# A timetable of the Mamba stage: dt and output products, C's turn, gates and z's SiLUs at other slots

## The chip, the core and the metric

The kernel runs on one NeuronCore of a Trainium2 chip. The metric is the device time of one launch in microseconds (us). Five engines work side by side, each through its own instruction stream in order, and meet only through semaphores: TensorE (PE in the views; matmuls and transposes into the eight banks of PSUM), VectorE (DVE), ScalarE (ACT), GpSimd (POOL) and SyncE (SP, which here only issues DMAs, its queue being SPq). The Mamba stage's data is fp32.

## The reference, cut to what matters

The input is x, 2 sequences of 4096 tokens by 256. It is normalised and modulated and goes through a Mamba layer forward and one backward in time; both results pass a sigmoid, are averaged, normalised and added to the residual; then an FFN with ternary weights follows. The Mamba layer is what the change touches:

```
xi, z = split(x @ in_proj.T)                 # 512 channels each
xi    = silu(causal_conv(xi) + conv_b)
dt, B, C = split(xi @ x_proj.T)              # 64, 16, 16 columns
dt    = softplus(dt @ dt_w.T + dt_b)
dA, dBx = exp(dt * A), dt * xi * B           # for each of 16 states
h     = dA * h + dBx                         # along time
y     = (sum over states of h * C) + xi * D
out   = (y * silu(z)) @ out_proj.T
```

## The kernel before, in words

The Mamba stage runs 32 bodies: two passes (backward, then forward in time) of 16 chunks, a chunk being 512 tokens of one sequence; chunks of the two sequences take turns. After it comes the FFN stage (from line 1497 on), which the change leaves alone.

A body has 32 **units** k. Units 0 to 15 are the 16 states of the first half of the channels, 16 to 31 those of the second half; a unit has two tiles m of 128 channels by 512 tokens. A body thus has 64 **slots** g = 2k + m. Each engine walks the slots in order, and beside the scan work of chunk n it does the front work of chunk n+1 and the tail work of chunk n-1, each piece at the slot that a table gives. The tables are written out by hand at the top of the file, `AT` (lines 43 to 50) for TensorE's slots, with fixed lags for the readers: ScalarE reads a front product `ACT_LAG` = 3 slots after its last step, VectorE gates `DVE_LAG` = 2 slots after the turn.

The scan work of a unit:

- ScalarE makes the decay exp(dt * A) of each tile (`decay`, L1145), into one of three PSUM banks; a decay of tile i waits until scan i-3 is over. Units 19, 22, 25, 28 and 31 (`A_UNITS`) are the other way about: the decay goes to SBUF, and the share dBx comes from TensorE as a product with a diagonal matrix (`fill_a`, L815), at slots 2k-2 and 2k-1.
- GpSimd makes dBx of the other units (`weigh_b`, L1283).
- VectorE scans (`scan`, L1400), a tile at a time.
- Four units later h is weighed with C: 12 units on GpSimd (L1294), 20 on VectorE (L1408); for these TensorE first spreads C over the partitions (`spread_c`, L850) into a single bank, which needs the weighing before it to be over.
- Five units later TensorE turns h and sums it over the states in PSUM (`turn_h`, L868). At the end of each half it adds xi * D (`turn_skip`, L880) and ScalarE copies the sum to `acc` (`evacuate`, L1099; slot 44 for the first half). The turn of the next unit waits for both copies.

The pieces that the tables place, with their jobs in two PSUM banks (`FB`, numbers in `BANK`), each job waiting until its bank's last job has been read:

- `J_X`, `J_CONV`, `J_B`: x part of in_proj, convolution, x_proj. ScalarE copies them; `xi_silu` (L1060) makes two SiLUs of 128x1024 at slots 24 and 31 (`AT_XI`).
- `J_C`: turn of B and C (L783), read by ScalarE (L1041) 3 slots later.
- `J_DT`: four dt products (L731), read by ScalarE twice each (L1048, L1049); then exp and ln at slots 48, 49, 53, 54.
- `J_Z`: z part of in_proj, copied by ScalarE (L1026) for the next chunk; `z_silu` (L1087) makes its SiLU for the chunk being scanned, at `AT_ZS`.
- `J_Y`: turn of `acc` to channels (L724), gated by VectorE with silu(z) (`gate`, L1377): two tiles for the first half of the channels, two (at slots 13 and 17 of the next body) for the second.
- `J_OUT`: two output products of four quarters each (`tail`, L835), one quarter a slot; ScalarE reads each with a tanh (L1111) 6 slots after it began; SP stores the chunk when both are read.

The exp and Silu functions lie in different table sets, so an ACT_TABLE_LOAD stands wherever ScalarE changes between them. Within a slot ScalarE does the decay first, then tail, then front, then xi's SiLU, then z's. Within a slot TensorE does spread and turn of h, then tail, the turns of y and u, `fill_a`, then front. The first chunk's front is made in a prologue of 64 slots of its own, where z's products stand at `FIRST_Z`.

Of the kernel before, what the change touches and what calls it, by code (L numbers as in the profile page):

```python
# [39 lines left out]
J_LN, J_X, J_CONV, J_B, J_DT, J_Z = (0, 1), (2, 3, 4, 5), (6, 7, 8, 9), 10, (11, 12, 13, 14), (15, 16, 17, 18)  # L40
J_Y, J_OUT, J_C = (19, 20, 21, 22), (23, 24), 25
J_UT = (26, 27)
AT = {J_LN: (0, 1), J_X: (3, 5, 7, 9), J_CONV: (11, 16, 20, 24), J_DT: (35, 40, 43, 49), J_Z: (50, 52, 56, 57),
      J_Y: (46, 47, 13, 17), J_OUT: (32, 38), J_UT: (26, 29)}
AT_LN, AT_X, AT_CONV, AT_DT, AT_Z, AT_Y, AT_OUT, AT_UT = (AT[j] for j in (J_LN, J_X, J_CONV, J_DT, J_Z, J_Y, J_OUT, J_UT))
AT_B, AT_C = 29, 37
NFB = 2
BANK = (0, 1, 0, 1, 0, 1, 0, 1, 0, 1, 1, 1, 1, 1, 1, 0, 1, 0, 1, 1, 0, 1, 0, 0, 0, 1, 0, 0)
START = {J_B: AT_B, J_C: AT_C, **{j: g for jobs, gs in AT.items() for j, g in zip(jobs, gs)}}
FIRST_Z = (33, 46, 38, 52)  # L50
FIRST_START = {**START, **dict(zip(J_Z, FIRST_Z))}
AT_ROWS = (16, 21, 26, 30, 32, 37, 41)
R_MOD, R_BANK = 3, 1
# [14 lines left out]
ND, NP = len(D_UNITS), len(P_UNITS)  # L68
ACT_LAG, DVE_LAG = 3, 2
EVAC = (44, 12)  # L70
AT_XI, AT_ZS = (24, 31), (5, 62)
AT_XN = 19
AT_EXP = (48, 53)
AT_LNP = (49, 54)
# [281 lines left out]
def mamba(nc, a, bank, ident, cols, mod, gain, norm_c, fcol, any_odd, passes, w1, w2, J, x_v, yb_v, yf_v, xn_v, b_dram,  # L356
# [11 lines left out]
    with ExitStack() as c:  # L368
# [46 lines left out]
        def job(ch, i):  # L415

            b = BANK[i]

            def count(jobs):
                return sum(BANK[k] == b for k in jobs)

            def before(jobs, start=START):
                return sum(BANK[k] == b and start[k] < start[i] for k in jobs)

            nf, nm, nt = count(FRONT), count(MID), count(TAIL)
            back = 1 if i in FRONT else 0 if i in MID else -1
            n = ch.number()
            body = None if n is None else n - back  # L430
            if body == -1:
                return b, before(FRONT, FIRST_START)
            more = len(AT_ROWS) if b == R_BANK and (body == NALL or body == NALL - 1 and i in MID) else 0
            off = nf - nt + before(MID) + before(TAIL) + before(FRONT)
            if body == 0:
                off += nt - before(TAIL)
            if body == NALL - 1:
                off -= before(FRONT)
            if body == NALL:
                off = -nt + before(TAIL)  # L440
            return b, ch.at(nf + nm + nt, off - back * (nf + nm + nt) + more)

        def row_job(e):

            last = Chunk(NPASS - 1, NC - 1, 1)
            return job(last, next(i for i in MID if BANK[i] == R_BANK))[1] - len(AT_ROWS) + e

        def wait_filled(eng, ch, i):
            b, k = job(ch, i)
            eng.wait_ge(fill[b], k + 1)  # L450
# [268 lines left out]
        def _(pe):  # L719
            def turn(i, src, ch):  # L720

                wait_free(pe, ch, i)
                for s in range(TS):
                    mm = pe.transpose(FB[BANK[i]][:, s * P:(s + 1) * P], src(s), ident[:, :])  # L724
                mm.then_inc(fill[BANK[i]], 1)

            def part(ch, i, k, kn, lhsT, rhs, rows=P):

                if k == 0:
                    wait_free(pe, ch, i)  # L730
                mm = pe.matmul(FB[BANK[i]][0:rows, :], lhsT, rhs, start=(k == 0), stop=(k == kn - 1))  # L731
                if k == kn - 1:
                    mm.then_inc(fill[BANK[i]], 1)

            def front(ch, g):
# [10 lines left out]
                for m in range(KI):  # L746
# [20 lines left out]
                    if g == AT_DT[m]:  # L767
                        if m == 0:
                            wait_drained(pe, ch, J_B)
                        part(ch, J_DT[m], 0, 1, w_dt[:, m * P:(m + 1) * P], dbB[0:DTR, :])  # L770
                    k = g - (FIRST_Z if ch.first() else AT_Z)[m]
                    if 0 <= k < KM:
# [201 lines left out]
        def _(act):  # L974
            def front(ch, g):
# [25 lines left out]
                for m in range(KI):  # L1001
# [15 lines left out]
                    if g == AT_CONV[m] + DCONV - 1:  # L1017
# [4 lines left out]
                                       bias=cv[:, COL_CB + m:COL_CB + m + 1]).then_inc(drain[b], 1)  # L1022
                    if g == (FIRST_Z if ch.first() else AT_Z)[m] + KM - 1:
                        wait_filled(act, ch, J_Z[m])
# [798 lines left out]
```

## Time and profile before

| | us |
|---|---|
| median of 3 runs (lowest, highest) | 4886.2 (4885.44, 4889.81) |
| profiled execution | 4887.08 |
| its span, first to last instruction | 4885.3 |
| mean granted TensorE clock | 0.984 |

| engine | busy us | share of the span |
|---|---|---|
| TensorE matmul | 4500.2 | 92% |
| VectorE | 3896.9 | 80% |
| GpSimd | 3321.8 | 68% |
| ScalarE | 3277.3 | 67% |

The Mamba stage fills about the first 3545 us. A row of a timeline shows: start, duration, engine, line, operation, tiles, and how many instructions in a row it merges; in brackets the idle time before it and who ended that. The next instruction may start up to 0.2 us before the end of the one before it, so the distance of two starts (the stride) is a little less than the duration.

### The profile page before, as it was taken

The numbers are of one execution on the slowest core, as the hardware profiler recorded it, in microseconds if no ns is written. First come the engines' busy times: TensorE is split into PE (matmuls) and PEld (weight loads), VectorE is DVE, ScalarE is ACT, GpSimd is POOL, SyncE is SP. The second block draws the span as 40 slices with busy tenths as digits, with TensorE's granted clock in tenths as the row PEclk, the third lists the DMA queues.
The fourth block names the chain that finished last, engine by engine and source line by source line (L and its number), as shares of the span: only waits on it lengthen the run. The fifth ranks groups of instructions, "written<-read, shape, count | busy, mean of one in ns | idle before, by whom it ended". The sixth has DMA issues, their size and how long they took to land. (4 is left out here: it accounts for less than half of the span.)

```text
span 4885.3 us, 67229 instructions
## 1 busy us (share of the span) xinstructions
PE 4500.2 (92%) x24932; PEld 3377.8 (69%) x24932; DVE 3896.9 (80%) x4126; ACT 3277.3 (67%) x5281; POOL 3321.8 (68%) x1559
## 2 busy tenths in 40 slices
PE   7899889999889889999999999999789999999999
PEld 3666666666666666666666666666678888888888
DVE  6999999999999989999999999999855444545452
ACT  7877777777777777777777777777534444444443
POOL 5999999999999999998999999989920000000000
PEclk9999999999999999999999999999999999999999
DMA  8544444444444444444444444444430101011000
GB/s 287 171 135 130 149 129 130 123 138 136 129 141 137 139 126 131 134 131 126 134 141 129 127 129 126 133 137 131 141 124 31 35 31 35 31 33 33 29 28 9
DMA packets 297737, 545.77 MB, mean 112 GB/s; under 512 B 101888, under 2 KB 186624, under 8 KB 262784
## 3 DMA queue, kind: packets, MB, share of 16 engines
q1 hardware_dynamic: 296512, 529.91, 35.7%
q10 hardware_dynamic: 896, 11.54, 0.7%
q8 instruction: 199, 3.26, 0.3%
q14 instruction: 130, 1.06, 0.1%
HBM read 502.77 MB, written 50.14 MB: 113 GB/s over the span
## 5 line engine op out<-in xcount | busy, mean ns | idle before, releaser
L1400 DVE TENSOR_TENSOR_SCAN m_h<-bank,m_state,m_dBx 128x512 f32<-128x512 f32 x1512 | 1847.7, 1263 | 34.0 <-ACT bank L1145 27.8
L868 PEld LDWEIGHTS bank<-ident,m_h 128*128 128x128 f32 x8192 | 982.6, 144 | 627.4 <-issue 373.8
L868 PE MATMUL bank<-ident,m_h 128*128 128x128 f32 x8192 | 1246.8, 279 | 117.2 <-DVE m_h L1408 84.7
L1294 POOL TENSOR_TENSOR m_h<-m_h,m_Cs 128x1024 f32<-128x1024 f32 x384 | 909.5, 2373 | 214.9 <-ACT m_state L1077 214.8
L1283 POOL TENSOR_TENSOR m_dBx<-u,m_Bs 128x1024 f32<-128x1024 f32 x432 | 1013.8, 2376 | 2.4 <-issue 0.6
L1283 POOL TENSOR_TENSOR m_dBx<-m_u,m_Bs 128x1024 f32<-128x1024 f32 x432 | 1013.1, 2372 | 3.4 <-DMA m_Bs<-b_dram 1.3
L1408 DVE TENSOR_TENSOR m_h<-m_h,bank 128x1024 f32<-128x1024 f32 x640 | 765.1, 1195 | 14.6 <-PE bank L850 14.4
L1145 ACT ACTIVATE bank<-m_dt,cols 128x512 f32<-128x512 f32 x864 | 588.8, 688 | 218.8 <-DVE m_h L1400 215.5
L1145 ACT ACTIVATE bank<-dt,cols 128x512 f32<-128x512 f32 x864 | 588.8, 688 | 200.0 <-DVE m_h L1400 196.7
L302 POOL TENSOR_TENSOR mvj<-mvj,norm_c 128x4 f32<-128x4 f32 x16 | 16.2, 1015 | 983.4 <-DVE mvj L263 983.4
L850 PEld LDWEIGHTS bank<-ident,m_Ct 128*128 128x128 f32 x2560 | 300.1, 140 | 529.9 <-DVE m_h L1408 350.5
L850 PE MATMUL bank<-ident,m_Ct 128*128 128x128 f32 x2560 | 411.3, 285 | 221.2 <-DVE m_h L1408 219.1
L731 PE MATMUL bank<-hT,w_in 128*128 128x512 f32 x1024 | 522.4, 599 | 7.8 <-ACT hT L998 4.1
L731 PE MATMUL bank<-xpre,diag 128*128 128x512 f32 x1024 | 524.4, 596 | 0.0
L1588 PE MATMUL bank<-gb,h 128*128 128x512 f32 x2048 | 468.3, 390 | 0.0
L1588 PE MATMUL bank<-ga,h 128*128 128x512 f32 x2048 | 467.9, 389 | 0.0
L1400 DVE TENSOR_TENSOR_SCAN m_h<-m_h,m_state,bank 128x512 f32<-128x512 f32 x280 | 350.9, 1269 | 144.9 <-ACT bank L1145 84.5
L1588 PEld LDWEIGHTS bank<-ga,h 128*128 128x128 f32 x2048 | 384.3, 188 | 80.8 <-DVE ga L1726 0.3
L1588 PEld LDWEIGHTS bank<-gb,h 128*128 128x128 f32 x2048 | 383.3, 188 | 78.9
L1726 DVE TENSOR_TENSOR ga<-raw,ga 128x512 fp32r<-128x512 f32 x256 | 178.2, 696 | 302.2 <-ACT raw L1663 300.8
L815 PE MATMUL bank<-m_dg,m_uT 128*128 128x128 f32 x2560 | 340.3, 276 | 0.0
L815 PEld LDWEIGHTS bank<-m_dg,m_uT 128*128 128x128 f32 x2560 | 313.3, 193 | 0.0
(176 smaller groups left out, 6003.3 us busy)
## 6 DMA issues: line engine op xcount, KB each, us to landing
m_Bs<-b_dram SPq DMA_DIRECT2D x256, 1024.0 KB, 5.2
m_Cs<-c_dram SPq DMA_DIRECT2D x384, 256.0 KB, 3.5
m_dg<-d_dram SPq DMA_DIRECT2D x160, 256.0 KB, 3.6
xx<-in_x SPq DMA_DIRECT2D x16, 512.0 KB, 4.9
xn_dram<-xx SPq DMA_DIRECT2D x16, 512.0 KB, 4.6
yb_dram<-m_ysb SPq DMA_DIRECT2D x16, 512.0 KB, 4.4
xx<-xn_dram SPq DMA_DIRECT2D x16, 512.0 KB, 3.8
x_dram<-m_ysb SPq DMA_DIRECT2D x16, 512.0 KB, 4.4
```

What stands on the lines that cost most here:

```text
L302: pool.tensor_tensor(mvj[:, :, 3], mvj[:, :, 2], norm_c[:, 1, :], ALU.pow).then_inc(S["join"], 1)
L731: mm = pe.matmul(FB[BANK[i]][0:rows, :], lhsT, rhs, start=(k == 0), stop=(k == kn - 1))
L815: mm = pe.matmul(DA[tile % NDA][:, s * P:(s + 1) * P], uT[:, s, m * P:(m + 1) * P], dg[:, n % NDG, s, :], start=True, stop=True)
L850: mm = pe.matmul(CB[:, t * P:(t + 1) * P], Ct[:, ch.batch, t, s:s + 1].broadcast_to((P, P)), ident[:, :], start=True, stop=True, is_transp ...
L868: mm = pe.matmul(YB[b][:, o:o + P], h[:, k % NH, m, tok:tok + P], ident[:, :], start=(s == 0 and o == 0), stop=False, is_transpose=True, s ...
L1145: act.activation(out, dt[ch.batch][:, m, :], ACT.Exp, scale=cols[:, ch.ps, col:col + 1]).then_inc(S["da"], 1)
L1283: pool.tensor_tensor(dBx[:, dbx_ring(ch, k) % NDBX, :, :], u[ch.batch][:, m, :], Bs[:, k // BP % 2, k % BP, :].unsqueeze(1).broadcast_to(( ...
L1294: pool.tensor_tensor(o, o, Cs[:, i % 2, :].unsqueeze(1).broadcast_to((P, 2, T)), ALU.mult).then_inc(S["weigh_p"], 1)
L1400: dve.tensor_tensor_scan(o, decays, share, initial, ALU.mult, ALU.add).then_inc(S["scan"], 1)
L1408: dve.tensor_tensor(o, o, CB[:, :].unsqueeze(1).broadcast_to((P, 2, T)), ALU.mult).then_inc(S["weigh_d"], 1)
L1588: return pe.matmul(out, lhsT, rhs, start=start, stop=stop)
L1726: dve.tensor_tensor(dst[:, 1], raw[:, j % XR, :], dst[:, 0].bitcast(F32), ALU.subtract).then_inc(S["lo"], 1)
```

## The change

It alters tables only. In a body: the first output product moves from slot 32 to 33 and the second from 38 to 44; the third dt product from 43 to 42 and the fourth from 49 to 46; C's turn from 37 to 38; the turns of the first half's y from 46 and 47 to 60 and 61, and with them VectorE's first two gates from 48 and 49 to 62 and 63; the second dt product uses bank 0 instead of 1; z's SiLUs move from slots 5 and 62 to 24 and 31, where xi's are. In the prologue the first chunk's second and third z products move from 46 and 38 to 48 and 37.

```diff
-AT = {J_LN: (0, 1), J_X: (3, 5, 7, 9), J_CONV: (11, 16, 20, 24), J_DT: (35, 40, 43, 49), J_Z: (50, 52, 56, 57),
-      J_Y: (46, 47, 13, 17), J_OUT: (32, 38), J_UT: (26, 29)}
+AT = {J_LN: (0, 1), J_X: (3, 5, 7, 9), J_CONV: (11, 16, 20, 24), J_DT: (35, 40, 42, 46), J_Z: (50, 52, 56, 57),
+      J_Y: (60, 61, 13, 17), J_OUT: (33, 44), J_UT: (26, 29)}
...
-AT_B, AT_C = 29, 37
+AT_B, AT_C = 29, 38
 NFB = 2
-BANK = (0, 1, 0, 1, 0, 1, 0, 1, 0, 1, 1, 1, 1, 1, 1, 0, 1, 0, 1, 1, 0, 1, 0, 0, 0, 1, 0, 0)
+BANK = (0, 1, 0, 1, 0, 1, 0, 1, 0, 1, 1, 1, 0, 1, 1, 0, 1, 0, 1, 1, 0, 1, 0, 0, 0, 1, 0, 0)
 START = {J_B: AT_B, J_C: AT_C, **{j: g for jobs, gs in AT.items() for j, g in zip(jobs, gs)}}
-FIRST_Z = (33, 46, 38, 52)
+FIRST_Z = (33, 48, 37, 52)
...
-AT_XI, AT_ZS = (24, 31), (5, 62)
+AT_XI, AT_ZS = (24, 31), (24, 31)
```

## Rows read from the trace of the kernel before

**Rows 1.** The page's slices: VectorE's busy tenths in 40 slices.

```profile
DVE  6999999999999989999999999999855444545452
```

**Rows 2.** Timeline of VectorE over one body; columns as told above.

```profile
2027.21 2.45 DVE L1400 TENSOR_TENSOR_SCAN m_h<-bank,m_state,m_dBx 128x512 f32<-128x512 f32 x2
...
2068.68 1.28 DVE L1400 TENSOR_TENSOR_SCAN m_h<-bank,m_state,m_dBx 128x512 f32<-128x512 f32 x1 [0.48 <-ACT bank L1145]
...
2080.31 2.45 DVE L1400 TENSOR_TENSOR_SCAN m_h<-bank,m_state,m_dBx 128x512 f32<-128x512 f32 x2
...
2088.90 1.22 DVE L1408 TENSOR_TENSOR m_h<-m_h,bank 128x1024 f32<-128x1024 f32 x1 [0.31 <-PE bank L850]
2090.26 2.58 DVE L1400 TENSOR_TENSOR_SCAN m_h<-m_h,m_state,bank 128x512 f32<-128x512 f32 x2
...
2101.80 2.58 DVE L1400 TENSOR_TENSOR_SCAN m_h<-m_h,m_state,bank 128x512 f32<-128x512 f32 x2 [3.13 <-ACT bank L1145]
...
2106.06 1.28 DVE L1400 TENSOR_TENSOR_SCAN m_h<-bank,m_state,m_dBx 128x512 f32<-128x512 f32 x1 [0.50 <-ACT bank L1145]
...
2109.56 0.67 DVE L1377 TENSOR_TENSOR m_z<-bank,m_z 128x512 f32<-128x512 f32 x1
...
2111.92 2.44 DVE L1400 TENSOR_TENSOR_SCAN m_h<-m_h,m_state,bank 128x512 f32<-128x512 f32 x2
...
2129.42 1.25 DVE L1400 TENSOR_TENSOR_SCAN m_h<-m_h,m_state,bank 128x512 f32<-128x512 f32 x1
2132.53 1.28 DVE L1400 TENSOR_TENSOR_SCAN m_h<-m_h,m_state,bank 128x512 f32<-128x512 f32 x1 [1.87 <-ACT m_h L1145]
...
2134.84 2.45 DVE L1400 TENSOR_TENSOR_SCAN m_h<-bank,m_state,m_dBx 128x512 f32<-128x512 f32 x2
```

**Rows 3.** Timeline of TensorE over the same body.

```profile
2084.83 1.03 PE L835 MATMUL bank<-m_w_out,m_z 128*128 128x256 f32 x4
...
2086.13 1.03 PE L835 MATMUL bank<-m_w_out,m_z 128*128 128x256 f32 x4
2087.09 1.12 PE L731 MATMUL bank<-m_dbB,m_w_dt 64*128 64x512 f32 x2
2088.14 0.65 PE L850 MATMUL bank<-ident,m_Ct 128*128 128x128 f32 x4
...
2089.07 1.06 PE L815 MATMUL bank<-m_dg,m_uT 128*128 128x128 f32 x8
...
2100.11 0.66 PE L868 MATMUL bank<-ident,m_h 128*128 128x128 f32 x4 [0.60 <-ACT m_acc L1099]
2100.60 1.06 PE L815 MATMUL bank<-m_dg,m_uT 128*128 128x128 f32 x8
...
2134.98 1.11 PE L850 MATMUL bank<-ident,m_Ct 128*128 128x128 f32 x4 [3.61 <-DVE m_h L1408]
```

**Rows 4.** Timeline of ScalarE over the body of rows 2.

```profile
2065.58 1.06 ACT L1060 ACTIVATE m_xi<-m_u 128x1024 f32<-128x1024 f32 x1
2066.66 1.28 ACT L1145 ACT_TABLE_LOAD   x1
2067.96 1.30 ACT L1145 ACTIVATE bank<-dt,cols 128x512 f32<-128x512 f32 x2
...
2079.47 0.69 ACT L1145 ACTIVATE bank<-dt,cols 128x512 f32<-128x512 f32 x1
...
2097.22 0.69 ACT L1048 ACTIVATE m_u<-bank,cols 128x512 f32<-128x512 f32 x1 [2.48 <-PE bank L731]
...
2098.99 1.07 ACT L1099 COPY m_acc<-bank 128x512 f32<-128x512 f32 x2
```

**Rows 5.** Timeline of SP's DMA queue over the same body.

```profile
2117.39 7.54 SPq L577 DMA_DIRECT2D m_Bs<-b_dram  x2
```

**Rows 6.** Timeline of GpSimd over the same body.

```profile
2129.35 6.97 POOL L1283 TENSOR_TENSOR m_dBx<-m_u,m_Bs 128x1024 f32<-128x1024 f32 x3
```

**Rows 7.** Timeline of TensorE, a body of the first pass.

```profile
1077.29 0.65 PE L850 MATMUL bank<-ident,m_Ct 128*128 128x128 f32 x4 [1.70 <-DVE m_h L1408]
```

## The prediction

> **What bounds the kernel now.** I read the page's shares first, then the timelines of VectorE, TensorE and ScalarE over one steady body (one chunk, 32 units of two scans, 64 slots g; slot 2k is the first half of unit k), then SP's and GpSimd's. The shares over the span hide two stages: VectorE's slices are at nine tenths nearly all through the Mamba stage and at four or five in the FFN stage behind it [rows 1], which isn't touched. So the body's length is what counts: VectorE's first scan of two successive bodies stands at 2027.21 and 2134.84, 107.6 us apart [rows 2]. VectorE's own work in it is 64 scans at a stride of 1.18, 20 weighings at 1.12 and 4 gates at 0.58, 100.2 us. The rest is five waits and small gaps behind them [rows 2]: 0.48 at 2068.68 (slot 25), 0.31 at 2088.90 with some 0.2 before 2090.26 (slots 37, 38), 3.13 at 2101.80 (slot 44), 0.50 at 2106.06 (slot 47), 1.87 at 2132.53 (slot 63). The view puts the 3.13 down to ScalarE's decay, but that is unit 22, whose share comes from a TensorE fill; this fill runs 2100.60 to 2101.66 [rows 3], and the scan starts 0.14 behind it. So slot 44 is TensorE's: the fill is late because of the products ahead of it in its order, the last wait before it being 0.60 for ScalarE's copies of acc. Slots 25 and 63 are ScalarE's: two table loads of 1.28 around a Silu of 1.06 hold the next decay back [rows 4]. A change is worth what it takes off these five, less the waits that it makes.
>
> **Part 1, z's SiLUs.** Slot 5's block (load, Silu, load) goes. VectorE doesn't wait there, so it brings 0. Slot 62's goes: VectorE's two scans of unit 31 stand 3.11 apart (2129.42, 2132.53) and need 1.18, so 1.93 comes back. At slots 24 and 31 z's Silu now follows xi's directly: I take no table load between them, so the block grows by one Silu, 1.06 less the 0.10 by which such instructions overlap, 0.96. At slot 24 VectorE waits already, so all of it is path: +0.96. At slot 31 the decay starts at 2079.47, lasts 0.69 and the scan starts at 2080.31 [rows 2, 4]: cover 0.1 at most, +0.91. Unit 16 starts 1.87 later than now. Bounds of the two together: 0.9 (the second hidden) to 7.0 (with 1.28 of loads kept on both sides of each Silu), taken 1.87, from the chain just read. ScalarE saves four loads, 5.1 us a body, beside other work. Here the load at 2066.66 lasts 1.28 and the next decay runs at 2067.96, 1.30 behind it [rows 4]. The Trainium skill's page "ScalarE: Activation LUTs", section "What ACT_TABLE_LOAD costs", adds a drain of 1.38 us to each load; by it ScalarE would save 10.7 us a body instead of 5.1 and the block at slot 24 would be about 6 us instead of 3.6 long. The trace does not agree, and decides.
>
> **Part 2, output and dt products before unit 19 (slots 32 to 38).** The first output product moves from slots 32-35 to 33-36. Its last quarter now stands between unit 14's spread and unit 19's fill. TensorE must first turn unit 12, whose weighing ends two scans and itself after unit 16's start: 2080.31 + 1.87 + 2.38 + 1.19 = 2085.75. From 2085.81 TensorE does: turn 0.49, quarter 0.86, turn 0.44, quarter 0.96, dt 1.05, spread 0.49, turn 0.44, quarter 0.86, in all 5.59 [rows 3] (strides: 2084.83 to 2086.13 for a quarter and a turn, 2086.13 to 2087.09, 2087.09 to 2088.14, 2088.14 to 2089.07). The fill starts at 2091.40, ends 2092.46, unit 19 is scanned from 2092.59 instead of 2090.26: +2.33. The 0.31 at slot 37 vanishes in this. Bounds: +1.6 (VectorE alone) to +2.4.
>
> **Part 3, slots 38 to 44.** C's turn goes from 37 to 38 (0.33 us, TensorE idle follows: 0). The second output product leaves slots 38-41, four quarters of 0.87, so TensorE is at the end of slot 41 about 2098.2 in spite of the lateness; it no longer bounds. What is late next is ScalarE: unit 20's first scan runs 2095.09 to 2096.3, decay 43 takes 0.62 to 2097.00, the dt product's two reads and decay 44 take 1.77 (2097.22 to 2098.99) [rows 4], the two acc copies 1.07, to 2099.84. TensorE resumes at 2099.89, not 2100.11. Unit 22 is scanned from 2101.58 instead of 2101.80: **-0.22**. So of the 3.5 us taken off TensorE nearly all pays for the 2.33.
>
> **Part 4, slots 42 to 50.** The third dt product comes to slot 42, between unit 22's two fills: the second fill starts 0.99 + 1.05 + 0.49 = 2.53 behind the first (2102.91, end 2103.97), the second scan at 2104.09, where now it is at 2103.10 (+0.99). ScalarE's reads at slot 45 are done by 2103.7, so the 0.50 at slot 47 goes. VectorE could start unit 25 at 2104.09 + 1.20 + 2.36 + 1.12 + 2.36 = 2111.13, the gates having left. But TensorE has, from 2102.91: fill 0.89, two turns and two quarters 2.60, spread 0.44, turn 0.43, quarter 0.96, dt 1.05, turn 0.49, quarter 0.86, turn 0.44, 8.16: fill of unit 25 2111.07 to 2112.13, scan 2112.26, the second 2113.58, unit 26 at 2114.78 against 2114.28 (2111.92 + 2.36): **+0.50**. ScalarE's decay 50 ends at 2111.8 behind the fourth dt reads, just hidden. Bounds: 0 to +1.2 (decay 50 late by 0.7).
>
> **Part 5, slots 50 to 63.** The gates stay two of 0.58, at slots 62 and 63 now; 1.17 is paid there, and 1.17 saved at 48 and 49 is in part 4. Their turns are ready, at slots 60 and 61. These add 0.87 to TensorE ahead of unit 31's second fill; I get the fills' ends at 2129.6 and 2131.4 and the scans at 2129.92 and 2131.70, hidden by 0.2. Next body: 2129.92 + 1.20 + 0.58 + 1.18 + 0.59 + 1.11 = 2134.58, now 2134.84: **-0.26 a body**. Bounds: that to +0.9, if TensorE is 0.8 later. The second output tile is read at slot 50 rather than 44, so SP, which issues in order, sends the store of y at some 2112.1, and behind it queue a C load, a diagonal load, the four diagonal stores and the next B load, which goes from 2117.39 to about 2118.9; GpSimd needs it at 2129.35 [rows 5, 6]. Hidden: 10 us less a landing of 5.2 by the page. The second dt product's other bank makes it wait for the first output tile's read, which is over 3 us before: 0. The first chunk's z products move by a slot or two in the prologue, where I give 0, with bounds of -2 and +2 us once.
>
> **Sum.** 31 bodies at -0.3 (the -0.26, and a trifle at slot 5) are -9.3; the last body, where TensorE's tail work is what VectorE waits for, -2. From the profiled execution, 4887.1 (span 4885.3 and 1.8 around it), that is 4875.8; from the median, 0.9 lower, **4875**. About 0.2%, 9.8 us, is what can be told from no change, so the likeliest case lies on this edge. The parts are differences of large terms: 1 us a body is 31 us.
>
> **Rivals.** *A: TensorE's relief counts in full.* If the SiLUs' lateness is absorbed ahead of unit 22 and the fills of 22 and 25 come in time: -2.5 at slot 44, -0.5 at 47, -1.9 at 63, +1.9, -3.0 a body, 4793. For it: the largest wait is TensorE's. Against it: the ScalarE chain and the third dt product above. Half of it gives 4835.
> *B: ScalarE's chain through decay 43, the dt reads and the acc copies decides.* From the acc copies' end TensorE runs with no break to unit 25, so each tenth of lateness there goes straight to the body's end. It is 0.22 ahead now; from 0.04 behind on the kernel is slower. If it comes 1 us later than worked out (another instruction of ScalarE in the chain, or turns at 60 and 61 that hold unit 31's fills): +0.7 a body, 4908. For it: all margins here are below 0.5. Against it: each link is a row.
> *C: TensorE's clock falls at new places.* After an idle of 3.61 four transposes took 1.11 (1.2 GHz), after one of 1.70 0.65 (2.4 GHz) [rows 3, 7]. The new idle stretches at slots 34 and 42 are 1.3 and 1.6. If they too let it fall, 3 us of path a body: 4975.
> *D: the two moves only exchange waits*, within 0.1 us a body: 4883 to 4889.
>
> **Chances.** Forecast (4860 to 4880) 0.34, A and half of it 0.16, D and the forecast's weak side 0.26, B 0.21, C 0.03. Range 4838 to 4912. Faster 0.48, same 0.29, slower 0.23.
>
> **What would show it.** In a steady body: no table load at slots 5 and 62; VectorE's wait at slot 25 near 1.4 and a new one near 0.9 at slot 32; about 1 us at slot 38, 0.65 at slot 44, 1.3 at 45, 1.1 at 50; no wait at 47 or 63; TensorE's clock low less often at the body's start, where its idle shrinks from 3.6 to about 1.5. The prediction is wrong if the wait at slot 32 is absent, if slot 44's stays over 1 us, or if a body is more than 1 us away from 107.3.

## The result, and the profile after

The changed kernel takes 4989.36 us (median of 4 runs, 4984.14 to 4993.17) against 4887.32 before (4 runs): a ratio of 1.0208, 95% interval 1.019 to 1.0225. It is 102 us slower, where 12 us faster was forecast, and outside the range of 4838 to 4912. The profiled execution has a span of 4989.7 us. From the page after:

```profile
PE 4511.3 (90%) x24932; PEld 3354.8 (67%) x24932; DVE 3903.8 (78%) x4126; ACT 3241.2 (65%) x5247; POOL 3324.5 (67%) x1559
```

No engine does notably more work: ScalarE is even 36 us less busy, with 34 instructions fewer. (Four table loads a body were to go, about 120 in all; that only 34 did is the first trace of what happened.) So the time is idle time, and the timeline of VectorE over one body shows where. These rows answer to [rows 2]; a body runs here from 2090.08 to 2201.50, 111.42 us against 107.63. (The body of [rows 2] is a long one: the kernel before has three of 107.62 or 107.63 in its second pass and most of 107.49.)

```profile
2090.08 2.45 DVE L1400 TENSOR_TENSOR_SCAN m_h<-bank,m_state,m_dBx 128x512 f32<-128x512 f32 x2
...
2132.35 1.28 DVE L1400 TENSOR_TENSOR_SCAN m_h<-bank,m_state,m_dBx 128x512 f32<-128x512 f32 x1 [1.42 <-ACT bank L1145]
...
2144.92 2.46 DVE L1400 TENSOR_TENSOR_SCAN m_h<-bank,m_state,m_dBx 128x512 f32<-128x512 f32 x2 [0.86 <-ACT bank L1145]
...
2155.33 2.58 DVE L1400 TENSOR_TENSOR_SCAN m_h<-m_h,m_state,bank 128x512 f32<-128x512 f32 x2 [1.00 <-PE bank L815]
...
2164.31 1.28 DVE L1400 TENSOR_TENSOR_SCAN m_h<-m_h,m_state,bank 128x512 f32<-128x512 f32 x1 [0.56 <-PE bank L815]
2166.81 1.28 DVE L1400 TENSOR_TENSOR_SCAN m_h<-m_h,m_state,bank 128x512 f32<-128x512 f32 x1 [1.23 <-PE bank L815]
...
2175.02 1.28 DVE L1400 TENSOR_TENSOR_SCAN m_h<-m_h,m_state,bank 128x512 f32<-128x512 f32 x1 [1.10 <-PE bank L815]
2177.16 1.28 DVE L1400 TENSOR_TENSOR_SCAN m_h<-m_h,m_state,bank 128x512 f32<-128x512 f32 x1 [0.86 <-ACT m_h L1145]
...
2184.85 1.28 DVE L1400 TENSOR_TENSOR_SCAN m_h<-bank,m_state,m_dBx 128x512 f32<-128x512 f32 x1 [1.75 <-ACT bank L1145]
...
2193.21 1.22 DVE L1408 TENSOR_TENSOR m_h<-m_h,bank 128x1024 f32<-128x1024 f32 x1 [1.25 <-PE bank L850]
...
2201.50 2.45 DVE L1400 TENSOR_TENSOR_SCAN m_h<-bank,m_state,m_dBx 128x512 f32<-128x512 f32 x2
```

Down to slot 50 the waits are those the prediction named, in place and in size: 1.42, 0.86, 1.00, 0.56, 1.23, 1.10 at slots 25, 32, 38, 44, 45, 50, and none at 47 and 63. Then stand three that it didn't have: 0.86 at slot 51, 1.75 at slot 55, and 1.25 ahead of unit 25's weighing, at slot 59. ScalarE's timeline over slots 47 to 55 shows the cause; compare what [rows 4] show of a table change.

```profile
2168.84 1.28 ACT L983 ACT_TABLE_LOAD   x1
2170.13 1.06 ACT L986 ACTIVATE m_u<-m_u 128x1024 f32<-128x1024 f32 x1
...
2173.80 0.71 ACT L1145 ACTIVATE m_h<-dt,cols 128x512 f32<-128x512 f32 x1
2174.53 1.28 ACT L1111 ACT_TABLE_LOAD   x1
2175.82 0.60 ACT L1111 ACTIVATE m_ysb<-bank 128x512 f32<-128x512 f32 x1
...
2176.40 0.73 ACT L1145 ACTIVATE m_h<-dt,cols 128x512 f32<-128x512 f32 x1
...
2179.89 1.28 ACT L989 ACT_TABLE_LOAD   x1
2181.19 1.06 ACT L989 ACTIVATE m_u<-m_u 128x1024 f32<-128x1024 f32 x1
...
2182.83 1.28 ACT L1145 ACT_TABLE_LOAD   x1
2184.13 0.69 ACT L1145 ACTIVATE bank<-dt,cols 128x512 f32<-128x512 f32 x1
```

The load at slot 48 brings a table set with both Exp and Ln, in which the kernel before stayed until slot 62. The second output product's Tanh (L1111), now at slot 50, isn't in it: one load for the Tanh, one for the Ln of slot 54, and one more for the decay behind the Ln. The first delays decay 51 (slot 51's wait), the other two delay decay 55 (slot 55's). The third wait has another link. TensorE idles for 2.03 while VectorE waits at slot 55, and behind that it runs at 1.2 GHz for some microseconds; TensorE's timeline from slot 56, and the same slot a body later:

```profile
2187.30 0.66 PE L868 MATMUL bank<-ident,m_h 128*128 128x128 f32 x4 [2.03 <-DVE m_h L1408]
2187.80 1.07 PE L731 MATMUL bank<-hT,w_in 128*128 128x512 f32 x2
2188.66 1.06 PE L868 MATMUL bank<-ident,m_h 128*128 128x128 f32 x4
2189.51 3.15 PE L731 MATMUL bank<-hT,w_in 128*128 128x512 f32 x4
2192.50 0.60 PE L850 MATMUL bank<-ident,m_Ct 128*128 128x128 f32 x4
...
2298.72 0.66 PE L868 MATMUL bank<-ident,m_h 128*128 128x128 f32 x4 [2.03 <-DVE m_h L1408]
2299.21 1.02 PE L731 MATMUL bank<-hT,w_in 128*128 128x512 f32 x2
2300.07 0.60 PE L868 MATMUL bank<-ident,m_h 128*128 128x128 f32 x4
2300.51 1.88 PE L731 MATMUL bank<-hT,w_in 128*128 128x512 f32 x4
```

In the first body four transposes take 1.06 instead of 0.60 and four matmuls 3.15 instead of 1.88 (the granted clock of 2188 to 2192 is 0.58), and unit 25's spread is late; in the second the clock stays at 2.4 GHz behind the same idle of 2.03. The bodies show what each is worth. SP's queue, stores of y:

```profile
2176.45 0.37 SPq L605 DMA_DIRECT2D x_dram<-m_ysb  x1
...
2287.87 0.37 SPq L605 DMA_DIRECT2D x_dram<-m_ysb  x1
...
2397.79 0.37 SPq L605 DMA_DIRECT2D x_dram<-m_ysb  x1
```

111.42, then 109.92. In the second pass, from its third body on, the bodies have one of these two lengths, in the first 112.98 or 111.49 (a body there has extra normalisation work). The difference, 1.49, is the clock. Of the 30 distances that hold all three loads 17 have it, wholly or nearly (1.41 to 1.50), and one, where the passes meet, has half of it. These are the 18 bodies in which the granted clock falls to 1.2 GHz as this idle ends or up to 1.4 us later; in the other 12 it stays at 2.4 GHz.

### The profile page after: what moved, and what is told of

Same layout as the page of the kernel before. It is cut to its first block and busy times, and to the rows that moved or that the text cites. A ratio compares the mean times of both kernels' runs of the same rounds, so it can differ in the third digit from the quotient of the medians.

```text
span 4989.7 us, 67195 instructions
## 1 busy us (share of the span) xinstructions
PE 4511.3 (90%) x24932; PEld 3354.8 (67%) x24932; DVE 3903.8 (78%) x4126; ACT 3241.2 (65%) x5247; POOL 3324.5 (67%) x1559
## 3 DMA queue, kind: packets, MB, share of 16 engines
q14 instruction: 130, 1.06, 0.1%
## 5 line engine op out<-in xcount | busy, mean ns | idle before, releaser
L850 PEld LDWEIGHTS bank<-ident,m_Ct 128*128 128x128 f32 x2560 | 287.4, 137 | 522.8 <-DVE m_h L1408 346.9
L850 PE MATMUL bank<-ident,m_Ct 128*128 128x128 f32 x2560 | 400.9, 279 | 200.5 <-DVE m_h L1408 197.4
L731 PE MATMUL bank<-hT,w_in 128*128 128x512 f32 x1024 | 546.3, 624 | 5.7 <-ACT hT L998 2.7
```

The source lines that it names most:

```text
L850: mm = pe.matmul(CB[:, t * P:(t + 1) * P], Ct[:, ch.batch, t, s:s + 1].broadcast_to((P, P)), ident[:, :], start=True, stop=True, is_transp ...
```

## The experiments

**1. The Tanh's function alone.** The change with a Copy in the place of the Tanh at slot 50.

```diff
-                                       ACT.Tanh, scale=0.5).then_inc(drain[b], 1)
+                                       ACT.Tanh if i == 0 else ACT.Copy, scale=0.5).then_inc(drain[b], 1)
```

> The changed kernel with its second output product read by a Copy instead of a Tanh at slot 50 (this leaves out the sigmoid of half the tokens). Theory T (tables): the Tanh now stands between the Exp of slot 48 and the Ln of slot 54, whose tables have no Tanh, and brings three loads of 1.28 in slots 50 to 55; with Copy they go and the body falls from 111.4 to about 107.4: 4875, between 4865 and 4890. Rival P (TensorE's order: output quarters and dt products before unit 25, gates' turns at 60 and 61): these stand as they are, so at least half of the loss stays: over 4940. Rival C (TensorE's clock falling after idle): stays, over 4940, and the low clock near slot 56 is seen again.

4879.65 (10 runs), ratio to before 0.9984 (0.9975 to 0.9993). VectorE's timeline, its waits over one body:

```profile
2067.07 1.28 DVE L1400 TENSOR_TENSOR_SCAN m_h<-bank,m_state,m_dBx 128x512 f32<-128x512 f32 x1 [1.42 <-ACT bank L1145]
2079.64 2.46 DVE L1400 TENSOR_TENSOR_SCAN m_h<-bank,m_state,m_dBx 128x512 f32<-128x512 f32 x2 [0.86 <-ACT bank L1145]
2090.05 2.58 DVE L1400 TENSOR_TENSOR_SCAN m_h<-m_h,m_state,bank 128x512 f32<-128x512 f32 x2 [1.00 <-PE bank L815]
2099.03 1.28 DVE L1400 TENSOR_TENSOR_SCAN m_h<-m_h,m_state,bank 128x512 f32<-128x512 f32 x1 [0.57 <-PE bank L815]
2101.53 1.28 DVE L1400 TENSOR_TENSOR_SCAN m_h<-m_h,m_state,bank 128x512 f32<-128x512 f32 x1 [1.22 <-PE bank L815]
2109.74 2.58 DVE L1400 TENSOR_TENSOR_SCAN m_h<-m_h,m_state,bank 128x512 f32<-128x512 f32 x2 [1.10 <-PE bank L815]
2174.30 1.28 DVE L1400 TENSOR_TENSOR_SCAN m_h<-bank,m_state,m_dBx 128x512 f32<-128x512 f32 x1 [1.43 <-ACT bank L1145]
```

All three unforeseen waits are gone, the six foreseen are left, the body is 107.23. Rivals P and C fall: TensorE's order is the same here and its time with it. The clock's fall was real but a consequence, of an idle that the loads had made. The body is 2.70 shorter than the changed kernel's undisturbed one (109.93), 4.19 shorter than the other.

**2. The Exp and Ln moved behind the Tanh.**

```diff
-AT_EXP = (48, 53)
-AT_LNP = (49, 54)
+AT_EXP = (51, 55)
+AT_LNP = (52, 56)
```

> The changed kernel with the Exp and Ln of dt moved from slots 48, 49, 53, 54 to 51, 52, 55, 56, so that the Tanh of slot 50 comes ahead of the table they need; nothing is left out. Theory T: three loads less a body, 4875 (4865 to 4892), perhaps 0 to 10 more for GpSimd getting dt 3 us later. Rival P and rival C: over 4940.

4915.46 (5 runs), ratio 1.0058 (1.0044 to 1.0071). 74 us of the loss go, but not all: outside both expectations. The three extra loads are gone, and a body is 108.3. Two waits are new, for decays 52 and 53. ScalarE's timeline behind unit 25:

```profile
2132.98 1.28 ACT L983 ACT_TABLE_LOAD   x1
2134.27 1.06 ACT L986 ACTIVATE m_u<-m_u 128x1024 f32<-128x1024 f32 x1
2135.24 0.68 ACT L1145 ACTIVATE bank<-dt,cols 128x512 f32<-128x512 f32 x1
2135.85 1.04 ACT L989 ACTIVATE m_u<-m_u 128x1024 f32<-128x1024 f32 x1
```

The load, Exp and Ln at slots 51 and 52 now follow the wait for unit 25's fill, when VectorE has no work stored up; at slots 48 and 49 VectorE had units 23 and 24 ahead of it. VectorE waits 0.68 and 0.18 there. I had counted GpSimd's lateness and not this.

**3. z's SiLUs alone**, on the kernel before.

```diff
-AT_XI, AT_ZS = (24, 31), (5, 62)
+AT_XI, AT_ZS = (24, 31), (24, 31)
```

> The kernel before with only z's SiLUs moved to slots 24 and 31. By the chain of the prediction: unit 16 starts 1.87 later, unit 19 1.47 later, this stays to slot 62, where 1.93 comes back: -0.46 a body, 4873 (4865 to 4882). Rival S (the SiLUs' blocks are what cost): +1 to +2 a body, 4917 to 4950.

4872.34 (6 runs), ratio 0.997 (0.9958 to 0.9982): a gain of 15 us, where the chain gave 14. A body is 107.00, 0.50 less than the 107.49 or 107.50 of most bodies before. Rival S falls.

**4. The suspected cost added to the kernel before.**

```diff
+                    if k == 50 and has(ch, 1):
+                        act.activation(warm[:, :], no_halo[:, 0, 0:1], ACT.Tanh)
```

> The kernel before with one extra Tanh of 128x1 on ScalarE at slot 50 of each body, into a tile that nothing reads. Theory T: three loads more between slots 50 and 55, decay 55 3.9 us later than now with 1 us of cover: +3 to +4 a body, 4980 to 5010. Rivals P and C: TensorE's order is that of before, so under 4910.

5027.24 (4 runs), ratio 1.0289 (1.0274 to 1.0305). (In its file the scan is line 1403, the decay 1146.) One instruction of 0.20 us costs 140 us, 4.5 a body; over what I expected by 17 to 47. ScalarE's timeline has the same three loads:

```profile
2183.66 1.28 ACT L1198 ACT_TABLE_LOAD   x1
2184.96 0.20 ACT L1198 ACTIVATE m_warm<-m_no_halo 128x1 f32<-128x1 f32 x1
...
2189.78 1.28 ACT L990 ACT_TABLE_LOAD   x1
...
2192.73 1.28 ACT L1146 ACT_TABLE_LOAD   x1
```

VectorE waits 2.91 at slot 55, 1.15 at unit 25's weighing, 0.25 at slot 51 and 0.3 more than before at slot 63. The 1.15 and the 0.3 are what my figure lacked, and they are the clock again. They stand in this body, where the clock is low behind the idle of slot 56, and not in a body of the first pass where it stays up; TensorE at slot 56 in either:

```profile
1297.52 0.66 PE L869 MATMUL bank<-ident,m_h 128*128 128x128 f32 x4 [3.18 <-DVE m_h L1411]
...
2197.20 1.12 PE L869 MATMUL bank<-ident,m_h 128*128 128x128 f32 x4 [3.19 <-DVE m_h L1411]
```

Ten bodies of the first pass in which it stays up are 3.2 to 3.9 longer than before, which is the 3 to 4 expected of the loads; the last 13 of the second pass, in which it falls, are 5.0 to 5.2 longer. Function, order and size are thus told apart: the loads alone, in the order of before, slow the kernel; the change's order without them doesn't.

**5. The Tanh made later.** The change, with a copy at slot 50 and the Tanh in place at slot 58; SP stores y behind the next chunk's first B loads.

```diff
+                        else:
+                            act.copy(ysb[:, 2:4, :], y).then_inc(drain[b], 1)
+                if g == AT_TANH:
+                    wait_drained(act, ch, J_OUT[1])
+                    o = ysb[:, 2:4, :]
+                    act.activation(o, o, ACT.Tanh, scale=0.5).then_inc(S["y_tanh"], 1)
```

> The changed kernel with its second output product copied at slot 50 and its Tanh made in place at slot 58, where one table load (1.28) is all it needs; the store of y goes behind the next chunk's first B loads. Nothing is left out. Theory T: body 107.2 to 107.5, 4880 (4875 to 4890). Rival (ScalarE has no room for a load and a Tanh at slot 58 either): over 4910.

4878.99 (11 runs), ratio 0.9983 (0.9974 to 0.9992). The change's timetable with nothing left out, and with 1 load where there were 3, is 110 us faster than as it was made and 8 faster than before: near the 4875 forecast.

**6. The dt products back at 43 and 49**, on kernel 5 (`J_DT: (35, 40, 43, 49)`).

> As the last kernel, with the third and fourth dt products back at slots 43 and 49. If the stretch from the acc copies to unit 25 is TensorE's, as the prediction counts it, the wait of 1.2 at slot 45 goes, but what decides is that one dt product (1.05) leaves the stretch: -1.05 a body, 4848 (4840 to 4858). Rival: ScalarE's reads of the third dt product, at slot 46 again, hold decay 47 and eat it: 4870 to 4885.

4879.56 (11 runs), ratio 0.9983 (0.9974 to 0.9992): no gain; the rival is right. VectorE's waits behind slot 44 (in kernels 5 to 9 the scan is line 1408, the decay 1153, the fill 816):

```profile
2105.48 1.28 DVE L1408 TENSOR_TENSOR_SCAN m_h<-bank,m_state,m_dBx 128x512 f32<-128x512 f32 x1 [0.51 <-ACT bank L1153]
...
2110.73 2.58 DVE L1408 TENSOR_TENSOR_SCAN m_h<-m_h,m_state,bank 128x512 f32<-128x512 f32 x2 [0.38 <-ACT m_h L1153]
...
2114.90 1.28 DVE L1408 TENSOR_TENSOR_SCAN m_h<-bank,m_state,m_dBx 128x512 f32<-128x512 f32 x1 [0.41 <-ACT bank L1153]
```

The 1.2 at slot 45 and the 1.1 at slot 50 are gone, as TensorE's count has it, but ScalarE now holds decays 47, 50 and 53: it reads the dt products at slots 46 and 52, in front of them. Here a TensorE chain gave way to a ScalarE chain of nearly the same length.

**7. The first output product back at slot 32**, on kernel 6 (`J_OUT: (32, 44)`).

> As the last one, with the first output product back at slot 32. By the prediction's chain the quarter ahead of unit 19's fill costs 0.86 and reaches the acc copies through unit 20's scan and decay 43: another -0.86 a body, 4822 (4812 to 4832). Rival: the 0.86 is idle time elsewhere: within 5 us of the kernel with the dt products back.

4853.14 (5 runs), ratio 0.9931 (0.9917 to 0.9944): 26 us less than kernel 6, 0.86 a body (106.28 against 107.14). The wait at slot 38 is gone. The rival falls. (4853 lies outside the range expected, since the 4822 was counted from a kernel 6 at 4848; the step itself, 0.86 a body, is what the chain gave.)

**8. z's SiLUs back at 5 and 62**, on kernel 7 (`AT_ZS = (5, 62)`).

> As the last one, with z's SiLUs back at slots 5 and 62. By the prediction's chain unit 22 comes 1.47 earlier and 1.93 is lost at slot 63: +0.46 a body, 14 us slower than with them at 24 and 31. Rival: with TensorE relieved the SiLUs behind the convolution's cost their full 1.87 against 1.93: no difference over 3 us.

4854.69 (5 runs), ratio 0.9932 (0.9918 to 0.9945): 1.5 us from kernel 7, within the runs' spread: the rival's number is right, but not its reason. The SiLUs behind the convolution's didn't cost 1.87: from slot 38 on kernel 8 is 1.48 earlier than kernel 7, as the chain has it (1.47). What was off is the 1.93 at slot 63: that scan waits 1.48 instead of the 1.87 that I took over from the kernel before, because the first gate, 0.58, now stands ahead of it and covers a part.

**9 and 10. Only the second SiLU moved**, on kernel 7 and on the kernel before (`AT_ZS = (5, 31)` in both).

> As the kernel with the first output product at 32, with z's first SiLU back at slot 5 (where VectorE has no wait) and the second left at 31 (slot 62's wait stays away). By the chain of the prediction the wait at slot 25 falls from 1.4 to 0.48, unit 16 starts 0.96 earlier and unit 22 with it: -0.9 a body, 4824 (4816 to 4836). Rival: TensorE or ScalarE swallow it before unit 22, as they did with the dt products: over 4842.

> The kernel before with only z's second SiLU moved, from slot 62 to 31. Unit 16 starts 0.91 later, TensorE takes in 0.4 of it up to unit 19, slot 63 gives 1.93 back: -1.4 a body, 4843 (4834 to 4856). Rival: the gain is only what moving both gave, about -15 us: 4868 to 4876.

4824.22 (4 runs), ratio 0.9874 (0.9859 to 0.989), and 4843.56 (5 runs), ratio 0.9911 (0.9898 to 0.9925). Both fall on the chain's figures (4824 and 4843), and both rivals fall. VectorE's waits in a body of kernel 9, the fastest of all:

```profile
2139.84 1.28 DVE L1408 TENSOR_TENSOR_SCAN m_h<-bank,m_state,m_dBx 128x512 f32<-128x512 f32 x1 [0.49 <-ACT bank L1153]
2152.40 2.46 DVE L1408 TENSOR_TENSOR_SCAN m_h<-bank,m_state,m_dBx 128x512 f32<-128x512 f32 x2 [0.85 <-ACT bank L1153]
2170.93 2.58 DVE L1408 TENSOR_TENSOR_SCAN m_h<-m_h,m_state,bank 128x512 f32<-128x512 f32 x2 [0.56 <-PE bank L816]
2175.19 1.28 DVE L1408 TENSOR_TENSOR_SCAN m_h<-bank,m_state,m_dBx 128x512 f32<-128x512 f32 x1 [0.50 <-ACT bank L1153]
2180.44 2.58 DVE L1408 TENSOR_TENSOR_SCAN m_h<-m_h,m_state,bank 128x512 f32<-128x512 f32 x2 [0.37 <-ACT m_h L1153]
2184.60 1.28 DVE L1408 TENSOR_TENSOR_SCAN m_h<-bank,m_state,m_dBx 128x512 f32<-128x512 f32 x1 [0.41 <-ACT bank L1153]
```

## Why the prediction was wrong

**The step that failed** is in part 5: "The second output tile is read at slot 50 rather than 44", of which the prediction followed only SP's store. It also passed by in part 4, where decay 50 is called "just hidden" and ScalarE's next steps are not written down. The reading is a Tanh; slot 50 lies between the Exp of slots 48 and 53 and the Ln of 49 and 54; and the text ahead of the prediction says that a load stands wherever ScalarE changes between the sets of Exp and Silu, without my asking which sets hold the Tanh. The runs put in its place: three loads, 2.70 a body (109.93 against 107.23 in experiment 1), and 1.49 more in 17 of the 18 bodies in which TensorE's clock falls. From the first scan to the last the two profiled executions are 110.8 apart: 30 bodies at 2.70 are 81.0, the clock in 18 of them 25.8, the last body 4.4, less 0.3 in the first; the medians are 110 apart. The Trainium skill's page "ScalarE: Activation LUTs", section "Table sets: the hidden batching unit", lists Tanh with the Exp set and names a set of Exp and Ln that it does not list it in. The traces agree with both: behind the Tanh's load at 2174.53 the decays and the Exp of slot 53 (2178.25) need none, and in experiment 4 one Tanh brings three loads. I used that page for a load's price and not for which functions share one.

**Part 1** was right. Unit 16 starts 1.87 later by the sum, by the traces 1.88 (experiment 1 against a body of 107.50 before), and the waits of 1.42 and 0.86 at slots 25 and 32 bear it out; alone the move gains 15 us (14 foreseen). Between the two SiLUs of a block no load stands. What was missed is that the first half of the move only costs: experiment 10 leaves it out and gains 44.

**Parts 2 and 3** were right: 1.00 at slot 38 (about 1 foreseen) and 0.56 at slot 44 (0.65), and the chain by which lateness at unit 19 reaches the acc copies gave the steps of experiments 7, 9 and 10 to 1 us.

**Part 4** was right for the change as made (1.23 at slot 45, 1.10 at slot 50 in experiment 1), but its account, that TensorE's stretch alone decides, was one-sided: experiment 6 shortened the stretch by 1.05 and gained 0.09 a body.

**Part 5's** gates were right: no wait at slots 61 to 63. Rival C named the clock, but for the idle at slots 34 and 42 (1.18 and 1.50 in the trace after), behind which it stayed at 2.4 GHz in the body shown; it fell behind an idle that no part had. At the body's start, where the prediction had it low less often, it is never low in the second pass of the trace after (the idle there is 1.87, about 1.5 foreseen). **The sum** is right link by link once the loads are out: against a body of 107.50 before, experiment 1's is later by 2.34 at slot 38 (2.33 foreseen), by -0.23 at slot 44 (-0.22), 0.98 at slot 45 (0.99), 0.51 at slot 52 (0.50), and at its end by -0.27 (-0.26). The 107.37 was counted from the long body of 107.63; experiment 1 has 107.23. Two slips stand in the rivals and decide nothing: half of A is 4840 and not 4835, and C's 3 us a body give 4979 and not 4975.

What stays open is why the clock falls behind one idle of 2.03 and not behind the next: no run was made on it. The clock's 1.49 is read from bodies of one trace that differ in it; no run holds the clock up.

## What to carry to other kernels

When an instruction of ScalarE is moved, write down the table set in force at its old and at its new place: between an Exp and a Ln that share a set, one foreign function of 0.2 us cost three loads, 3.84 us of ScalarE, of which 2.70 in the change and about 3.5 in experiment 4 came onto the path, where the engine feeds a scan with a ring of three. (Naming the shared set again right behind the Tanh might save one of the three; it was not tried.) Within a timetable of in-order engines, follow each wait to the next engine, as the sum here did, but follow the moved instruction's kind first and its queue second. And split a paired move: one half of the SiLUs' brought all the gain, the other took two thirds of it back.

## What the runs showed of the hardware that I had not expected

One function of another set between an Exp and a Ln costs three loads and not two: the load at 2179.89, for the Ln alone, was followed by another at 2182.83 for the next decay's Exp, although the set loaded at slot 48 served both.

TensorE's clock fell to 1.2 GHz behind an idle of 2.03 in 18 of 30 bodies, while in the kernel before it stayed at 2.4 GHz behind one of 3.61 in the body from 2242 (the transposes at 2242.47 took 0.65, the next 0.60) and fell behind one of 3.61 at [rows 3]: the length of the idle alone doesn't tell. Its price depends on the place: at a body's start it cost nothing in the body from 2134.84 (107.50 long) and 0.14 at most (the body of 107.63, where it is low from 2025.8 to 2032.6), at slot 56 it cost 1.49.
